# Reordered sums on POOL, one tap moved off PE in every other tile, and the clamps moved to ACT, in the first stage of a fused vision block

## The chip, the cores and the metric

The kernel runs on one core of one Trainium2 chip. The metric is the device time of one execution in microseconds (us). An execution has a span, from the first to the last recorded instruction, and a slightly longer time of its own. Five engines run their instruction streams in parallel, each in program order: PE (TensorE, matmuls into PSUM), DVE (VectorE), ACT (ScalarE), POOL (GpSimd) and SP (which issues the transfers here). They meet only at semaphores: an instruction waits until a counter has reached a value, and adds to another counter when it is done.

## The reference, cut to what matters

The input x has the shape (2, 64, 256, 256): two batches of 64 channels. The change touches only the first stage, which computes the first residual and the input of the recurrent layer behind it:

```
x  = x + depthwise_conv_3x3(_ln_c(x), L0_conv_kernel)      # nine taps per channel, padding 1
t  = _to_tokens(x)                                         # (batch, 65536, 64)
Wx = einsum('bti,hi->bth', _ln_t(t), W)                    # then batch-norm statistics of Wx
```

Here `_ln_c` and `_ln_t` subtract the mean over the 64 channels of a pixel and divide by the root of the variance over them. Behind this stage come the recurrence, an attention with a 1x1 convolution, a mixture of experts, and the output, which all stay as they are.

## The kernel before, in words

The 128 partitions hold batch times channel, and the free axis holds the pixels. The first stage works in tiles of 512 pixels (two image rows), of which there are NT = 128; four tiles make a block, which is the unit of the loads and of the layer-norm statistics. The stage is a software pipeline written out by hand. Every engine loops over steps t, and in step t it does its part of the tile g = t - lag, with one lag for each part: SQ = -4 (squares of the loaded x), CENTER = 5 (centring matmul, and the scaling on DVE), TAPS = 8 (tap matmuls on PE, tap products on ACT, their sums on POOL), SUMS = 9 (tap sums on DVE), FINISH = 10 (the last sum on POOL, which writes the new x), SQ1 = 10 (squares of the new x on ACT), PROJECT = 18 and SCALE = 19. The order inside a step is the order of the lines of that engine's loop.

The nine taps of the convolution are shared out. Of each tile PE does taps 3, 4 and 5 as matmuls with diagonal matrices into the PSUM tile `pst` (L385). DVE adds taps 6, 7 and 8 (L543), the last one into `acc`. ACT makes the products of taps 0, 1 and 2 in `prod` (named tap_products, L454), one buffer for each of the three, so that the product n of a tile can be written only when POOL has added product n of the tile before. POOL adds the three products to x in the buffer `xr` (named x_and_products, three of them, L485), each sum needing the one in front of it, and then adds `acc` in `finish` (L492), which writes x_ring.

The layer norms take two rounds of statistics per block, one for the loaded x (layer 0) and one for the new x (layer 1): PE means over channels of x and of its square (L368, L374), ACT the square of the mean (L432), DVE variance and clamp at zero (L550, L557), ACT logarithm and exponential, which make the reciprocal root (L439, L443, in the function `rsqrt`). The result goes to DRAM and comes back spread over the channels (L316, L325). A round stands in every second step. In the loop of ACT, `rsqrt` comes first in such a step, then the first product, the square of the mean, the other two products, the square of a loaded tile, and last the square of the new x (`square(1, g)`, L425), which waits for `finish` of the same step:

```
if l == 0:
    act.wait_ge(*loaded_x(k))
else:
    act.wait_ge(x1_ready, g + 1)
```

Of the kernel before, what the change touches and what calls it, by code (L numbers as in the profile page):

```python
# [10 lines left out]
ALU = mybir.AluOpType  # L11
# [11 lines left out]
NT = N // TILE  # L23
# [44 lines left out]
def build_program(nc, x, conv_k, ffn_w, ffn_v, gamma, beta, q_w, q_b, kv_w, kv_b, proj_w, proj_b,  # L68
# [4 lines left out]
    with stack:  # L73
# [144 lines left out]
        with ExitStack() as ph:  # L218
# [1 line left out]
            XSLOTS = 8  # L220
            RT = 8
            XR = 3
            NP, ND = len(ACT_TAPS), len(DVE_TAPS)
            X = sb("x_ring", [P, XSLOTS, BLOCK], F32, ph)
            xn = sb("xn", [P, 2 * RT + 2, PITCH], F32, ph)
            u = sb("wx", [P, 2, BLOCK], F32, ph)
# [70 lines left out]

            def wide(ps):
                return ps[:, :].rearrange("p (r w) -> p r w", w=W)

            @blk.sync
            def _(sp):
# [52 lines left out]
            @blk.tensor  # L355
            def _(pe):
                def stats_of(l, k):


                    n = round_of[l, k]  # L360
                    if l == 0:
                        pe.wait_ge(*loaded_x(k))
                    else:
                        pe.wait_ge(x1_ready, TPB * (k + 1))
                    if n:
                        pe.wait_ge(msq_done, n)
                    for j in range(TPB):
                        m = pe.matmul(psm[32 * j:32 * j + 32, :], stat32[:, :], x_tile(TPB * k + j), start=True, stop=True)  # L368
                    m.then_inc(mean_ready, 1)
                    pe.wait_ge(squared[l], TPB * (k + 1))  # L370
                    if n:
                        pe.wait_ge(clamped, n)
                    for j in range(TPB):
                        m = pe.matmul(pse[32 * j:32 * j + 32, :], stat32[:, :], sq[l][:, j, :], start=True, stop=True)  # L374
                    m.then_inc(second_ready, 1)

                def tap_sums(g):
                    pe.wait_ge(normed, min(g + 2, NT))
                    pe.wait_ge(pads_ready, 1)
                    if halos[g + 1]:  # L380
                        pe.wait_ge(halo, halos[g + 1])
                    if g >= 2:
                        pe.wait_ge(acc_step, ND * (g - 1))
                    for n, t in enumerate(PE_TAPS):
                        m = pe.matmul(wide(pst[g % 2]), taps[:, n * P:(n + 1) * P], tap_rows(g, t),  # L385
                                      start=(n == 0), stop=(n == len(PE_TAPS) - 1))
                    m.then_inc(taps_ready, 1)

                def center_x(g):
                    k = g // TPB  # L390
                    pe.wait_ge(*loaded_x(k))
                    if g >= 2:
                        pe.wait_ge(normed, g - 1)
                    pe.matmul(psc[g % 2][:, :], center, x_tile(g), start=True, stop=True).then_inc(centered, 1)  # L394

                def project(g):
                    pe.wait_ge(x1_ready, g + 1)
                    if g >= 2:
                        pe.wait_ge(u_ready, g - 1)
                    pe.matmul(psw[g % 2][:, :], wcT[:, :], x_tile(g), start=True, stop=True).then_inc(wx_ready, 1)  # L400

                for t in range(0, STEPS_A):
                    for l in range(2):
                        if (k := block_at(t, STATS[l])) is not None:
                            stats_of(l, k)
                    if (g := tile_at(t, CENTER)) is not None:
                        center_x(g)
                    if (g := tile_at(t, TAPS)) is not None:
                        tap_sums(g)
                    if (g := tile_at(t, PROJECT)) is not None:  # L410
                        project(g)

            @blk.scalar
            def _(act):
# [18 lines left out]

                def rsqrt(l, k):
                    n = round_of[l, k]
                    act.wait_ge(clamped, n + 1)
                    if n:
                        act.wait_ge(rstd_ready, n)
                    act.activation(ln[:, :], var[:, :], ACT.Ln, bias=(eps_c, eps_t)[l]).then_inc(ln_done, 1)  # L439
                    act.wait_ge(ln_done, n + 1)  # L440
                    if n >= 2:
                        act.wait_ge(rstd_out[n % 2], 32 * (n // 2))
                    act.activation(rstd[:, n % 2, :], ln[:, :], ACT.Exp, scale=-0.5).then_inc(rstd_ready, 1)  # L443

                def tap_product(g, n):
                    if n == 0:
                        act.wait_ge(normed, min(g + 2, NT))
                        act.wait_ge(pads_ready, 1)
                        if halos[g + 1]:
                            act.wait_ge(halo, halos[g + 1])  # L450
                    if g >= 1:
                        act.wait_ge(product_added, NP * (g - 1) + n + 1)
                    t = ACT_TAPS[n]
                    act.activation(prod[:, n, :, :], tap_rows(g, t), ACT.Copy,  # L454
                                   scale=kk[:, t:t + 1]).then_inc(products, 1)
# [19 lines left out]
            @blk.gpsimd  # L475
            def _(pool):
                pool.memset(xn[:, :, :].rearrange("p r w -> p (r w)"), 0.0).then_inc(pads_ready, 1)

                def add_product(g, n):
                    if n == 0 and g >= XR:  # L480
                        pool.wait_ge(x1_ready, g - XR + 1)
                    pool.wait_ge(products, NP * g + n + 1)
                    if n:
                        pool.wait_ge(product_added, NP * g + n)
                    pool.tensor_tensor(xr[:, g % XR, :], prod[:, n, :, :].rearrange("p r w -> p (r w)"),  # L485
                                       xr[:, g % XR, :] if n else x_tile(g), ALU.add).then_inc(product_added, 1)

                def finish(g):

                    pool.wait_ge(product_added, NP * (g + 1))  # L490
                    pool.wait_ge(acc_step, ND * (g + 1))
                    pool.tensor_tensor(x_tile(g), acc[:, g % 2, :, :].rearrange("p r w -> p (r w)"),  # L492
                                       xr[:, g % XR, :], ALU.add).then_inc(x1_ready, 1)

                for t in range(TAPS, STEPS_A):
                    if (g := tile_at(t, FINISH)) is not None:
                        finish(g)
                    if (g := tile_at(t, TAPS)) is not None:
                        for n in range(NP):
                            add_product(g, n)  # L500

            @blk.vector
            def _(dve):
                dve.wait_ge(pads_ready, 1)

                def norm_x(g):
# [3 lines left out]
                    if g >= RT:  # L510
                        done = g - RT + 2
                        dve.wait_ge(taps_ready, done)
                        dve.wait_ge(products, NP * done)
                        dve.wait_ge(acc_step, ND * done)
                    ps, scale = wide(psc[g % 2]), rb[0][:, k % 2, cols_of(g % TPB)].rearrange("p (r w) -> p r w", w=W)
                    if q == 0 and g:
                        dve.tensor_tensor(xn[:, 2 * RT + 1, 1:W + 1], ps[:, 0, :], scale[:, 0, :], ALU.mult).then_inc(halo, 1)
# [4 lines left out]
                def below_the_last_row():  # L522
                    done = NT - RT
                    dve.wait_ge(taps_ready, done)
                    dve.wait_ge(products, NP * done)
                    dve.wait_ge(acc_step, ND * done)
                    dve.memset(xn[:, 2 * RT + 1, 1:W + 1], 0.0).then_inc(halo, 1)

                def tap(g, n):
# [3 lines left out]
                        if halos[g + 1]:  # L533
                            dve.wait_ge(halo, halos[g + 1])
                    else:
                        dve.wait_ge(acc_step, ND * g + n)
                    out = wide(pst[g % 2])
                    if n == ND - 1:
                        if g >= 2:
                            dve.wait_ge(x1_ready, g - 1)  # L540
                        out = acc[:, g % 2, :, :]
                    t = DVE_TAPS[n]
                    dve.scalar_tensor_tensor(out=out, in0=tap_rows(g, t), scalar=kk[:, t:t + 1], in1=wide(pst[g % 2]),  # L543
                                             op0=ALU.mult, op1=ALU.add).then_inc(acc_step, 1)

                def variance(l, k):
# [1 line left out]
                    dve.wait_ge(second_ready, n + 1)  # L548
                    dve.wait_ge(msq_done, n + 1)
                    dve.tensor_tensor(pse[:, :], pse[:, :], msq[:, :], ALU.subtract).then_inc(var_done, 1)  # L550

                def clamp(l, k):
                    n = round_of[l, k]
                    dve.wait_ge(var_done, n + 1)
                    if n:
                        dve.wait_ge(ln_done, n)
                    dve.tensor_scalar(var[:, :], pse[:, :], 0.0, None, ALU.max).then_inc(clamped, 1)  # L557

                def scale_wx(g):
                    k = g // TPB  # L560
# [15 lines left out]
                for t in range(0, STEPS_A):  # L576
# [11 lines left out]
                        tap(g, 1)  # L588
                    if (g2 := tile_at(t, SCALE + TPB)) is not None:
                        statistics(g2)  # L590
                    for l, k in rounds:
                        clamp(l, k)
                    if g is not None:
                        tap(g, 2)
                    if (g := tile_at(t, CENTER)) is not None:
                        norm_x(g)


        with ExitStack() as ph:
# [1340 lines left out]
```

## Time and profile before

| | us |
|---|---|
| median of three runs | 1922.44 (1921.51 to 1926.3) |
| time of the profiled execution | 1924.74 |
| its span | 1922.9 |
| first product sum of tile 2 to that of tile 127, both on POOL | 666.0 |
| first stage, until its last instruction on DVE or ACT | about 757 |

A busy share of an engine over the span mixes stages with different limits, so this change is read from the stretch in which the first stage runs evenly, from about 50 to 725 us, and from single steps inside it. A granted clock of 1.00 is TensorE's full 2.4 GHz, and 0.50 is 1.2 GHz; a value between them is a mean over the stretch.

### The profile page before, as it was taken

How to read it: one execution, taken by the hardware profiler on the slowest of the kernel's cores; microseconds unless marked ns; L12 is line 12 of the kernel's file. 1: busy time of each engine (PE TensorE's matmuls, PEld its weight loads, DVE VectorE, ACT ScalarE, POOL GpSimd, SP SyncE). 2: the span in 40 equal slices, each digit the busy share in tenths (PEclk: the TensorE clock that was granted, in tenths of full speed). 3: DMA queues.
4: the chain of work that ended last, by engine and by line, in shares of the span. 5: the costliest groups of instructions: out<-in, count | busy, mean ns of one | idle time of the engine just before them, and what ended most of it. 6: DMA issues, size and time to landing. Idle time of an engine off the chain costs nothing. (4 is left out here: it accounts for less than half of the span.)

```text
span 1922.9 us, 24399 instructions
## 1 busy us (share of the span) xinstructions
PE 1556.5 (81%) x5627; PEld 648.4 (34%) x5627; DVE 1435.2 (75%) x2312; ACT 1238.3 (64%) x2178; POOL 1450.8 (75%) x1070
## 2 busy tenths in 40 slices
PE   4899999999999993698886679999999999816100
PEld 1333333333333331365553333333333333206000
DVE  1689999999999985498887547999999999951000
ACT  2777777777777751487875458889888888610000
POOL 2999999999999991058787129999999999901670
PEclk8999999999999996799988779999999999955555
DMA  4578888887888664989996527888888887570111
GB/s 152 163 230 254 251 234 256 251 254 234 253 254 252 192 192 152 313 278 373 368 391 269 219 45 209 287 287 287 285 284 275 278 286 246 192 179 13 2 2 1
DMA packets 114478, 429.81 MB, mean 224 GB/s; under 512 B 46720, under 2 KB 51744, under 8 KB 69280
## 3 DMA queue, kind: packets, MB, share of 16 engines
q1 hardware_dynamic: 92656, 423.78, 69.1%
q10 hardware_dynamic: 18736, 4.29, 1.5%
q8 instruction: 49, 0.80, 0.2%
q0 software_dynamic: 2944, 0.18, 0.1%
q14 instruction: 93, 0.76, 0.1%
HBM read 257.89 MB, written 170.01 MB: 223 GB/s over the span
## 5 line engine op out<-in xcount | busy, mean ns | idle before, releaser
L454 ACT ACTIVATE tap_products<-xn,kk 128x512 f32<-128x512 f32 x384 | 275.0, 718 | 156.6 <-POOL x_and_products L485 149.4
L485 POOL TENSOR_TENSOR x_and_products<-tap_products,x_and_products 128x512 f32<-128x512 f32 x256 | 327.1, 1278 | 41.5 <-POOL x_and_products L485 3.5
L385 PE MATMUL pst<-xn,taps 128*128 128x512 f32 x768 | 351.2, 592 | 0.0
L913 DVE SCALAR_TENSOR_TENSOR pss<-region,bn,pss 128x256 f32<-128x256 f32 x432 | 196.3, 489 | 67.4 <-PE pss L807 64.8
L1495 POOL TENSOR_SCALAR exp_q<-exp_q 128x512 f32<-128x512 f32 x128 | 189.3, 1479 | 73.3 <-ACT exp_q L1446 73.3
L852 POOL TENSOR_TENSOR x_block<-x_block,region 128x2048 f32<-128x2048 f32 x28 | 155.3, 5545 | 110.8 <-ACT region L839 88.5
L543 DVE SCALAR_TENSOR_TENSOR pst<-xn,kk,pst 128x512 f32<-128x512 f32 x256 | 192.2, 751 | 60.4 <-PE pst L385 60.2
L385 PEld LDWEIGHTS pst<-xn,taps 128*128 128x128 f32 x768 | 145.3, 189 | 186.3 <-issue 186.1
L1490 POOL TENSOR_TENSOR sq_norm<-x_ring 128x512 f32<-128x512 f32 x128 | 188.6, 1473 | 5.6 <-DVE x_ring L1542 1.7
L485 POOL TENSOR_TENSOR x_and_products<-tap_products,x_ring 128x512 f32<-128x512 f32 x128 | 163.4, 1277 | 19.2 <-ACT tap_products L454 19.2
L425 ACT ACTIVATE sq<-x_ring 128x512 f32<-128x512 f32 x256 | 157.6, 622 | 16.7 <-POOL x_ring L492 10.1
L1502 POOL TENSOR_TENSOR q_z<-q_map,z_inv 128x512 f32<-128x512 f32 x128 | 163.9, 1281 | 0.0
L492 POOL TENSOR_TENSOR x_ring<-acc,x_and_products 128x512 f32<-128x512 f32 x128 | 163.3, 1276 | 0.0
L807 PE MATMUL pss<-region,vT 128*128 128x256 f32 x480 | 137.5, 411 | 18.4 <-ACT region L839 18.2
L568 DVE TENSOR_TENSOR wx<-psw,rstd_wide 128x512 f32<-128x512 f32 x128 | 137.4, 1073 | 17.1 <-DMA rstd_wide<-rstd_scratch 10.9
L1379 PE MATMUL ps_denominator<-q_map,dT 128*128 128x512 f32 x256 | 138.5, 623 | 9.7 <-DVE q_map L1536 8.4
L1373 PE MATMUL ps_query<-x_ring,qcT 128*128 128x512 f32 x256 | 140.4, 632 | 4.0 <-DVE query L1527 4.0
L394 PE MATMUL psc<-x_ring,cst 128*128 128x512 f32 x256 | 140.1, 630 | 3.4 <-DVE xn L520 3.4
L400 PE MATMUL psw<-x_ring,wcT 128*128 128x512 f32 x256 | 132.9, 603 | 11.6 <-DVE wx L568 11.6
L807 PE MATMUL pss<-warm_state,vT 128*128 128x256 f32 x352 | 108.5, 431 | 40.2 <-ACT warm_state L839 22.1
L839 ACT ACTIVATE region<-pss,bn 128x256 f32<-128x256 f32 x256 | 116.6, 474 | 29.4 <-DVE pss L913 28.7
L1452 ACT ACTIVATE ln_d<-ps_denominator,cols 128x512 f32<-128x512 f32 x128 | 86.8, 678 | 73.2 <-PE ps_denominator L1379 73.0
(246 smaller groups left out, 2954.1 us busy)
## 6 DMA issues: line engine op xcount, KB each, us to landing
rstd_wide<-rstd_scratch SPq DMA_DIRECT2D x128, 512.0 KB, 7.2
x_ring<-in_x SPq DMA_DIRECT2D x32, 1024.0 KB, 5.3
x_scratch<-x_ring SPq DMA_DIRECT2D x32, 1024.0 KB, 4.3
xl_scratch<-wx SPq DMA_DIRECT2D x32, 1024.0 KB, 8.7
region<-xl_scratch SPq DMA_DIRECT2D x32, 1024.0 KB, 11.4
x_ring<-x_scratch SPq DMA_DIRECT2D x32, 1024.0 KB, 5.3
rstd_of_channels<-rstd_scratch SPq DMA_DIRECT2D x64, 512.0 KB, 7.5
out<-x_ring SPq DMA_DIRECT2D x32, 1024.0 KB, 6.6
```

The costliest lines, as they stand in the source:

```text
L385: m = pe.matmul(wide(pst[g % 2]), taps[:, n * P:(n + 1) * P], tap_rows(g, t), start=(n == 0), stop=(n == len(PE_TAPS) - 1))
L425: act.activation(sq[l][:, g % TPB, :], x_tile(g), ACT.Square).then_inc(squared[l], 1)
L454: act.activation(prod[:, n, :, :], tap_rows(g, t), ACT.Copy, scale=kk[:, t:t + 1]).then_inc(products, 1)
L485: pool.tensor_tensor(xr[:, g % XR, :], prod[:, n, :, :].rearrange("p r w -> p (r w)"), xr[:, g % XR, :] if n else x_tile(g), ALU.add).then ...
L492: pool.tensor_tensor(x_tile(g), acc[:, g % 2, :, :].rearrange("p r w -> p (r w)"), xr[:, g % XR, :], ALU.add).then_inc(x1_ready, 1)
L543: dve.scalar_tensor_tensor(out=out, in0=tap_rows(g, t), scalar=kk[:, t:t + 1], in1=wide(pst[g % 2]), op0=ALU.mult, op1=ALU.add).then_inc(a ...
L807: pe.matmul(ps_at(r, j), vT[:, :], before, start=True, stop=True).then_inc(carried, 1)
L852: pool.tensor_tensor(in_chunks(x1_x2), in_chunks(x1_x2), y, ALU.add).then_inc(added, 1)
L913: dve.scalar_tensor_tensor(out=ps_at(r, j), in0=u, scalar=gain_w, in1=ps_at(r, j), op0=ALU.mult, op1=ALU.add).then_inc(summed, 1)
L1490: pool.tensor_tensor(sq[1][:, g % SQSLOTS[1], :], x_tile(g), x_tile(g), ALU.mult).then_inc(squared[1], 1)
L1495: pool.tensor_scalar(e, e, 1.0, None, ALU.min).then_inc(clipped, 1)
L1502: pool.tensor_tensor(qz[:, g % 2, :], qm[:, g % QSLOTS, :], zr[:, g % 2, :], ALU.mult).then_inc(qz_ready, 1)
```

## The change

On POOL, a step now reads: first product of tile t-8, third product of tile t-9, second product of tile t-8, and then `finish` of tile t-10. Before, `finish` of tile t-10 stood first, and the three products of tile t-8 followed. ACT's waits for a free product buffer and POOL's waits for its own sums go by the new order of counting (`added_no`). In odd tiles PE does only taps 3 and 4, and DVE does taps 5, 6, 7 and 8, the fourth behind `norm_x`. The clamp of the variance moves from DVE to ACT, as a Relu at the head of `rsqrt`. The order of the rest of ACT's loop, the lags and the buffers stay.

```diff
+            added_no = {}
+            for g in range(NT + 1):
+                for tile, n in ((g, 0), (g - 1, 2), (g, 1)):
+                    if 0 <= tile < NT:
+                        added_no[tile, n] = len(added_no) + 1
+
+            def pe_taps(g):
+                return PE_TAPS[:2] if g % 2 else PE_TAPS
+
+            def dve_taps(g):
+                return PE_TAPS[2:] + DVE_TAPS if g % 2 else DVE_TAPS
...
                 def rsqrt(l, k):
                     n = round_of[l, k]
+                    act.wait_ge(var_done, n + 1)
+                    if n:
+                        act.wait_ge(ln_done, n)
+                    act.activation(var[:, :], pse[:, :], ACT.Relu).then_inc(clamped, 1)
                     act.wait_ge(clamped, n + 1)
...
                     if g >= 1:
-                        act.wait_ge(product_added, NP * (g - 1) + n + 1)
+                        act.wait_ge(product_added, added_no[g - 1, n])
...
                     if n:
-                        pool.wait_ge(product_added, NP * g + n)
+                        pool.wait_ge(product_added, added_no[g, n - 1])
...
                 for t in range(TAPS, STEPS_A):
+                    if (g := tile_at(t, TAPS)) is not None:
+                        add_product(g, 0)
+                    if (g := tile_at(t, TAPS + 1)) is not None:
+                        add_product(g, 2)
+                    if (g := tile_at(t, TAPS)) is not None:
+                        add_product(g, 1)
                     if (g := tile_at(t, FINISH)) is not None:
                         finish(g)
-                    if (g := tile_at(t, TAPS)) is not None:
-                        for n in range(NP):
-                            add_product(g, n)
...
-                def clamp(l, k):
-                    n = round_of[l, k]
-                    dve.wait_ge(var_done, n + 1)
-                    if n:
-                        dve.wait_ge(ln_done, n)
-                    dve.tensor_scalar(var[:, :], pse[:, :], 0.0, None, ALU.max).then_inc(clamped, 1)
...
-                    for l, k in rounds:
-                        clamp(l, k)
                     if g is not None:
                         tap(g, 2)
-                    if (g := tile_at(t, CENTER)) is not None:
-                        norm_x(g)
+                    if (g3 := tile_at(t, CENTER)) is not None:
+                        norm_x(g3)
+                    if g is not None and len(dve_taps(g)) == 4:
+                        tap(g, 3)
```

## Rows read from the trace of the kernel before

**Rows 1.** The windows view: busy us of each engine, granted clock, DMA.
```profile
100.00:200.00 100.00, 100.00 (x335) 38.95 (x334) 90.06 (x133) 76.58 (x122) 94.41 (x76) 1.00 0.82 240
```
**Rows 2.** The timeline of POOL: start, us, engine, line and operation.
```profile
55.33 1.27 POOL L485 TENSOR_TENSOR x_and_products<-tap_products,x_ring 128x512 f32<-128x512 f32 x1
...
86.33 1.27 POOL L492 TENSOR_TENSOR x_ring<-acc,x_and_products 128x512 f32<-128x512 f32 x1
87.56 1.27 POOL L485 TENSOR_TENSOR x_and_products<-tap_products,x_ring 128x512 f32<-128x512 f32 x1
88.98 1.27 POOL L485 TENSOR_TENSOR x_and_products<-tap_products,x_and_products 128x512 f32<-128x512 f32 x1
90.39 1.27 POOL L485 TENSOR_TENSOR x_and_products<-tap_products,x_and_products 128x512 f32<-128x512 f32 x1
91.61 1.28 POOL L492 TENSOR_TENSOR x_ring<-acc,x_and_products 128x512 f32<-128x512 f32 x1
...
721.35 1.28 POOL L485 TENSOR_TENSOR x_and_products<-tap_products,x_ring 128x512 f32<-128x512 f32 x1
```
**Rows 3.** The view of waits from 100 to 700 us: total, times, longest.
```profile
ACT tap_products L454 <- POOL x_and_products L485: 133.1, 212, 0.9
DVE pst L543 <- PE pst L385: 47.1, 56, 1.9
...
ACT sq L425 <- POOL x_ring L492: 3.6, 7, 0.5
```
**Rows 4.** The timeline of PE: one centring (x2) and one tile's taps (x6).
```profile
309.19 1.13 PE L394 MATMUL psc<-x_ring,cst 128*128 128x512 f32 x2
310.15 2.74 PE L385 MATMUL pst<-xn,taps 128*128 128x512 f32 x6
```
**Rows 5.** The timeline of ACT, two steps; x2 is two in a row.
```profile
71.08 1.23 ACT L425 ACTIVATE sq<-x_ring 128x512 f32<-128x512 f32 x2
72.22 0.71 ACT L439 ACTIVATE ln<-var,cols 128x512 f32<-128x512 f32 x1
72.96 0.63 ACT L443 ACTIVATE rstd<-ln 128x512 f32<-128x512 f32 x1
73.50 0.71 ACT L454 ACTIVATE tap_products<-xn,kk 128x512 f32<-128x512 f32 x1
74.11 0.58 ACT L432 ACTIVATE mean_squared<-ps_mean 128x512 f32<-128x512 f32 x1
```
**Rows 6.** The timeline where ACT releases POOL, and a square ahead of a product.
```profile
42.77 0.72 ACT L454 ACTIVATE tap_products<-xn,kk 128x512 f32<-128x512 f32 x1 [3.68 <-DVE xn L520]
43.57 1.26 POOL L485 TENSOR_TENSOR x_and_products<-tap_products,x_ring 128x512 f32<-128x512 f32 x1 [19.25 <-ACT tap_products L454]
47.81 0.62 ACT L425 ACTIVATE sq<-x_ring 128x512 f32<-128x512 f32 x1
48.33 1.32 ACT L454 ACTIVATE tap_products<-xn,kk 128x512 f32<-128x512 f32 x2
```
**Rows 7.** The timeline near the stage's end, where POOL's last sum releases ACT.
```profile
714.84 1.27 POOL L492 TENSOR_TENSOR x_ring<-acc,x_and_products 128x512 f32<-128x512 f32 x1
716.14 0.63 ACT L425 ACTIVATE sq<-x_ring 128x512 f32<-128x512 f32 x1 [0.50 <-POOL x_ring L492]
```
**Rows 8.** The lines view, 100 to 700 us: the clamp.
```profile
L557 DVE TENSOR_SCALAR var<-ps_second 128x512 f32<-128x512 f32 x56 | 37.9, 676 | 0.0
```
**Rows 9.** The timeline of the stage's tail: the last round but one.
```profile
722.71 0.63 ACT L443 ACTIVATE rstd<-ln 128x512 f32<-128x512 f32 x1
732.81 1.03 DVE L568 TENSOR_TENSOR wx<-psw,rstd_wide 128x512 f32<-128x512 f32 x1 [4.20 <-DMA rstd_wide<-rstd_scratch]
```
**Rows 10.** The windows view where PE is not always busy.
```profile
745.00:750.00 5.00, 2.16 (x3) 1.10 (x4) 3.06 (x5) 0.00 (x0) 0.00 (x0) 0.50 0.57 215
960.00:980.00 20.00, 14.22 (x54) 10.32 (x54) 17.41 (x31) 12.27 (x28) 14.96 (x5) 0.83 1.01 378
```

More of the change, by code:

```diff
@@ L222, in build_program @@
             XR = 3
-            NP, ND = len(ACT_TAPS), len(DVE_TAPS)
+            NP = len(ACT_TAPS)
             X = sb("x_ring", [P, XSLOTS, BLOCK], F32, ph)
@@ L299, in wide, with acc_steps @@
                 return ps[:, :].rearrange("p (r w) -> p r w", w=W)
+            added_no = {}
[7 more added lines that the diff above has]
+                return PE_TAPS[2:] + DVE_TAPS if g % 2 else DVE_TAPS
+            def acc_steps(tiles):
+                return sum(len(dve_taps(g)) for g in range(tiles))
             @blk.sync
@@ L382, in tap_sums @@
                     if g >= 2:
-                        pe.wait_ge(acc_step, ND * (g - 1))
-                    for n, t in enumerate(PE_TAPS):
+                        pe.wait_ge(acc_step, acc_steps(g - 1))
+                    for n, t in enumerate(pe_taps(g)):
                         m = pe.matmul(wide(pst[g % 2]), taps[:, n * P:(n + 1) * P], tap_rows(g, t),
-                                      start=(n == 0), stop=(n == len(PE_TAPS) - 1))
+                                      start=(n == 0), stop=(n == len(pe_taps(g)) - 1))
                     m.then_inc(taps_ready, 1)
@@ L488, in finish @@
                 def finish(g):
-                    pool.wait_ge(product_added, NP * (g + 1))
-                    pool.wait_ge(acc_step, ND * (g + 1))
+                    pool.wait_ge(product_added, added_no[g, NP - 1])
+                    pool.wait_ge(acc_step, acc_steps(g + 1))
                     pool.tensor_tensor(x_tile(g), acc[:, g % 2, :, :].rearrange("p r w -> p (r w)"),
@@ L513, in norm_x @@
                         dve.wait_ge(products, NP * done)
-                        dve.wait_ge(acc_step, ND * done)
+                        dve.wait_ge(acc_step, acc_steps(done))
                     ps, scale = wide(psc[g % 2]), rb[0][:, k % 2, cols_of(g % TPB)].rearrange("p (r w) -> p r w", w=W)
@@ L525, in below_the_last_row @@
                     dve.wait_ge(products, NP * done)
-                    dve.wait_ge(acc_step, ND * done)
+                    dve.wait_ge(acc_step, acc_steps(done))
                     dve.memset(xn[:, 2 * RT + 1, 1:W + 1], 0.0).then_inc(halo, 1)
@@ L535, in tap @@
                     else:
-                        dve.wait_ge(acc_step, ND * g + n)
+                        dve.wait_ge(acc_step, acc_steps(g) + n)
                     out = wide(pst[g % 2])
-                    if n == ND - 1:
+                    if n == len(dve_taps(g)) - 1:
                         if g >= 2:
@@ L541, in tap @@
                         out = acc[:, g % 2, :, :]
-                    t = DVE_TAPS[n]
+                    t = dve_taps(g)[n]
                     dve.scalar_tensor_tensor(out=out, in0=tap_rows(g, t), scalar=kk[:, t:t + 1], in1=wide(pst[g % 2]),
```

## The prediction, made before the changed kernel was run

> **What bounds the kernel now.** I read four views, in this order. The windows view shows how full each engine is while the first stage runs evenly [rows 1]: PE is busy for all of 100 us at the full clock, POOL for 94.4, DVE for 90.1, ACT for only 76.6. Two engines are candidates. The timeline of POOL then shows what the 5.6 us that are not busy are made of [rows 2]. `finish` at 86.33 and the sum behind it at 87.56 lie 1.23 us apart, so independent sums follow each other at that pitch. The sums at 87.56, 88.98 and 90.39, each needing the one in front, lie 1.42 and 1.41 us apart: a dependence costs 0.19 us. A tile is thus 1.23 + 1.42 + 1.41 + 1.22 = 5.28 us on POOL with no slack anywhere. From the first sum of tile 2 (55.33) to that of tile 127 (721.35) it is 666.0 us for 125 tiles, 5.33 each [rows 2]. POOL sets the pace; PE, whose busy share is full, stands close behind and is no slower than 5.33 per tile.
>
> The third view is the waits [rows 3]. ACT's products waited for POOL 212 times, 133.1 us together: ACT has slack, and it stands in front of the products. The wait that matters below is the small one: ACT's square of the new x waited for POOL's `finish` 7 times in 600 us, 3.6 us together. It was cheap because `finish` opened POOL's step. The fourth view, ACT's timeline, gives the prices of the pieces.
>
> **The change part by part.**
>
> *The order on POOL.* Only pairs that follow directly pay the 0.19. In the new order none of the four sums needs the product sum in front of it; the first sum of tile g still waits until `finish` of tile g-3 has freed its buffer, and that is now the instruction directly ahead. By itself a step would be 3 x 1.23 + 1.42 = 5.11 us, a gain of 0.22 on 5.33, or 27 us over 125 tiles. That gain needs a POOL that never waits for ACT.
>
> *What the order does to ACT.* Here I follow one loop through both programs. POOL's step ends with `finish` of tile g-2. ACT's step ends with the square of that same tile, which waits for it. ACT is in order, so the first product of tile g+1 stands behind that square, and POOL has nothing to do until it is there. Before, `finish` of g-2 was done before the first sum of tile g, some 4 us earlier, and this path had slack. Now the path is closed with no slack:
>
> - first sum to the end of `finish`: three pitches of 1.23 and one duration of 1.27 [rows 2], 4.96 us;
> - `finish` to the square: it ends at 714.84 + 1.27 = 716.11 and the square starts at 716.14 [rows 7], 0.03;
> - square to the product behind it: 47.81 to 48.33 [rows 6], 0.52;
> - product: 0.72, and release of POOL from 42.77 + 0.72 = 43.49 to 43.57 [rows 6], 0.08.
>
> Sum: 6.31 us for a step in which ACT has nothing else there. POOL idles 1.35 of them.
>
> *The statistics inside that loop.* `rsqrt` opens ACT's step in every second step, between the square and the product, so in the new order it lies on the path too. The second square of the pair at 71.08 starts at about 71.69 and the logarithm at 72.22, so 0.53; logarithm to exponential 72.22 to 72.96, 0.74; exponential to product 72.96 to 73.50, 0.54 [rows 5]. The Relu in front of it reads PSUM as the square of the mean does (0.58 [rows 5]) and its result is waited for as the exponential waits for the logarithm (0.03), so 0.61. Square to product becomes 0.53 + 0.61 + 0.74 + 0.54 = 2.42 instead of 0.52, which adds 1.90 us; such a step takes 8.21. No Relu is in the trace of before. Its lower bound is the 0.52 at which a square passes on [rows 6], its upper the 0.72 of a product; I take 0.58, the row that reads the same PSUM shape. Before, the clamp stood on DVE (676 ns each [rows 8]) off the path.
>
> *The sum over the stage.* The loop acts between the first sum of tile 2 and that of tile 127, 125 times. The steps 11 to 135 hold 29 rounds of layer 0 (steps 14, 18, ... 126) and 30 of layer 1 (16, 20, ... 132), so 59 `rsqrt`. That is 125 x 6.31 + 59 x 1.90 = 788.8 + 112.1 = 900.9 us against 666.0: +234.9.
>
> *The tail.* The `rsqrt` of the last round but one stands in step 136. Before it ended at 722.71 + 0.63 = 723.34, 1.99 us after the last tile's first sum, and the chain of transfer and scaling hangs on it (732.81, released by the transfer [rows 9]). Now it comes behind the square of tile 125: 4.96 + 0.03 + 0.53 + 0.61 + 0.74 + 0.63 = 7.50 us after that sum. The tail is 5.5 us longer. In the last round nothing precedes the Relu, and leaving DVE's order gives back some 0.6. I take +5.
>
> *The other parts.* Moving a tap costs nothing here, and gains nothing. DVE gets one tap and loses one clamp per two tiles; at 90% of 5.33 us per tile [rows 1] it does about 4.8 us of work in a step of 7.2. PE loses two matmuls per two tiles, (2.74 - 1.13) / 4 = 0.40 each [rows 4]: at most 10.66 - 0.80 = 9.86 us of work in 14.4. The cover for both is the loop above; without it DVE and PE would each set some 5 us per tile. The new wait on ACT holds back the products and, in every second step, PE's second-moment matmuls, which need the Relu of the round before; PE's taps of that step are used by DVE a step later and by POOL two steps later, which leaves several us.
>
> Prediction: 1924.74 + 234.9 + 5 = 2164.6, say 2165 us. The profiled execution lies 2.3 above the median, which the range covers.
>
> **Weighing the clock.** With PE a third idle, its clock can fall. The row nearest to that load is 960 to 980 us: busy 14.22 of 20, granted clock 0.83 [rows 10]; at 745 to 750, busy 2.16 of 5, it was 0.50. At 0.83, 9.86 us of work take 11.9, still inside 14.4. The Trainium skill (TensorE: Matmul & The Clock Gate, Part 1) says that the throttled state is the default and that activity lifts it. By the row the sum stays 2165; by that rule, taken to its end, see the second rival.
>
> **The rivals.**
>
> *Slower than that: PE at half clock becomes the bound.* The two tiles' 9.86 us double to 19.7 if every matmul runs at 1.2 GHz, and 62.5 pairs make 1232 us, +566, so 2496. It decides from the point where more than 14.4 / 9.86 - 1 = 46% of PE's work is done at the low level. At 60% the pair takes 15.8 and the total is 2250. For it: PE will pause in every pair of tiles. Against it: a PE that is behind stops pausing, and at such loads the clock stays above 0.8 [rows 10]. The skill's rule above names this cause.
>
> *Slower, but less: only the third product closes a loop.* It waits for a sum that now stands behind the first sum of the next tile: 1.23 + 1.27 + 0.03 + 0.62 (product to square) + 2 x 0.52 + 0.72 + 0.08 = 4.99, under POOL's 5.11, and 6.89 with `rsqrt`. 66 x 5.11 + 59 x 6.89 = 743.8, with the tail some 2008. This would hold if the square did not wait for `finish` of its own step; both lags are 10, so I see no room for it.
>
> *Faster: the loop doesn't close.* If the products were ready ahead of POOL, the step would be 5.11 and the time 1925 - 27 = 1898. It decides where the first product is made before `finish` ends. For it speak only ACT's 23% of idle time [rows 1] and the small wait of the square [rows 3]; against it, that this wait was small because of the very order that changes.
>
> **How the numbers follow.** Loop through `finish` as summed, 0.84, own range 2148 to 2210: the low end takes off 0.1 per step for releases that overlap more, the high end adds 0.1 for a square that passes on at a product's pitch (0.62), 0.09 for a slower release, 0.14 for each Relu, and up to 15 for pauses behind a slower PE. Half-clock PE 0.06, third product only 0.04, faster 0.04, no change 0.02. My range is 2142 to 2215. The chances below are those of faster by over 0.3%, within 0.3%, and slower by over 0.3%, which is about the smallest step that a measurement of this kernel tells from no change.
>
> **What would show it.** Right: POOL's busy share in the even stretch at some 70%, with an idle of 1.35 us before the first sum of each tile, and 3.25 in every second one, released by ACT's product; ACT's square released by POOL's `finish` some 125 times, 1.2 us each; first sum of tile 2 to tile 127 about 901 us; nothing changed behind the stage but its start. Wrong: first sums 5.1 us apart (no loop), or 5.1 and 6.9 (third product), or POOL idle behind DVE's `acc` with a granted clock of 0.6 or less (PE). An idle time well over 1.35 without `rsqrt` would mean that a release or the pitch of ACT is mis-sized.

## The result, and the profile after

The changed kernel takes 2171.21 us (median of four executions, 2165.34 to 2171.81), against 1924.37 (four executions) for the kernel before. The ratio is 1.1275, with a 95% interval of 1.1257 to 1.1294. It was forecast at 2165, with a range of 2142 to 2215. The profiled execution took 2171.58 us at a span of 2169.8.

In the code of the changed kernel the lines of the stage are L505 (the three product sums on POOL), L512 (the last sum), L474 (tap products on ACT), L441 (squares), L455 (the Relu), L459 and L463 (logarithm and exponential) and L566 (DVE's taps). The timeline of POOL answers to [rows 2]; in brackets stands the idle time ahead and who ended it.

```profile
56.42 1.27 POOL L505 TENSOR_TENSOR x_and_products<-tap_products,x_ring 128x512 f32<-128x512 f32 x1 [2.62 <-ACT tap_products L474]
...
303.58 1.27 POOL L505 TENSOR_TENSOR x_and_products<-tap_products,x_ring 128x512 f32<-128x512 f32 x1 [3.32 <-ACT tap_products L474]
304.80 2.50 POOL L505 TENSOR_TENSOR x_and_products<-tap_products,x_and_products 128x512 f32<-128x512 f32 x2
307.26 1.26 POOL L512 TENSOR_TENSOR x_ring<-acc,x_and_products 128x512 f32<-128x512 f32 x1
309.94 1.28 POOL L505 TENSOR_TENSOR x_and_products<-tap_products,x_ring 128x512 f32<-128x512 f32 x1 [1.42 <-ACT tap_products L474]
311.18 2.51 POOL L505 TENSOR_TENSOR x_and_products<-tap_products,x_and_products 128x512 f32<-128x512 f32 x2
313.62 1.28 POOL L512 TENSOR_TENSOR x_ring<-acc,x_and_products 128x512 f32<-128x512 f32 x1
318.23 1.28 POOL L505 TENSOR_TENSOR x_and_products<-tap_products,x_ring 128x512 f32<-128x512 f32 x1 [3.32 <-ACT tap_products L474]
...
965.45 1.28 POOL L505 TENSOR_TENSOR x_and_products<-tap_products,x_ring 128x512 f32<-128x512 f32 x1 [1.42 <-ACT tap_products L474]
```

The dependences between neighbouring sums are gone, as intended: the two sums that make up an "x2" take 2.50 us together, 1.23 from start to start, where a pair took 2.68 before (88.98 to 91.66 in [rows 2]). In exchange POOL now idles ahead of every first sum, 1.42 us in one step and 3.32 in the next. A step is 6.36 us or 8.29 us. From tile 2 to tile 127 it is 909.0 us, against 666.0.

ACT's timeline over the same two steps shows what POOL waits for; it answers to [rows 5].

```profile
306.10 0.72 ACT L474 ACTIVATE tap_products<-xn,kk 128x512 f32<-128x512 f32 x1 [1.57 <-POOL x_and_products L505]
306.73 0.61 ACT L441 ACTIVATE sq<-x_ring 128x512 f32<-128x512 f32 x1
308.56 0.63 ACT L441 ACTIVATE sq<-x_ring 128x512 f32<-128x512 f32 x1 [1.22 <-POOL x_ring L512]
309.10 1.32 ACT L474 ACTIVATE tap_products<-xn,kk 128x512 f32<-128x512 f32 x2
...
314.94 0.63 ACT L441 ACTIVATE sq<-x_ring 128x512 f32<-128x512 f32 x1 [1.22 <-POOL x_ring L512]
315.48 0.58 ACT L455 ACTIVATE var<-ps_second 128x512 f32<-128x512 f32 x1
316.09 0.72 ACT L459 ACTIVATE ln<-var,cols 128x512 f32<-128x512 f32 x1
316.85 0.63 ACT L463 ACTIVATE rstd<-ln 128x512 f32<-128x512 f32 x1
317.38 0.71 ACT L474 ACTIVATE tap_products<-xn,kk 128x512 f32<-128x512 f32 x1
```

Follow one turn. POOL's last sum ends at 307.26 + 1.26 = 308.52. The square starts at 308.56, the first product at 309.10, it ends at 309.82, and POOL starts at 309.94. In the other kind of step, Relu, logarithm and exponential stand between square (314.94) and product (317.38). ACT waits for POOL and POOL waits for ACT, in turn, and neither is full: the windows view, which answers to [rows 1], and the view of waits from 100 to 900 us, which answers to [rows 3].

```profile
100.00:200.00 100.00, 76.85 (x232) 26.79 (x231) 64.42 (x94) 57.66 (x95) 67.83 (x55) 0.89 0.56 169
500.00:600.00 100.00, 77.53 (x234) 27.20 (x233) 67.37 (x100) 58.25 (x97) 67.79 (x55) 0.88 0.60 180
```

```profile
POOL x_and_products L505 <- ACT tap_products L474: 257.2, 109, 3.3
ACT tap_products L474 <- POOL x_and_products L505: 200.5, 110, 2.1
...
ACT sq L441 <- POOL x_ring L512: 133.1, 109, 1.7
```

The square's wait was met 7 times in 600 us before and 109 times in 800 us now, once in every step. No engine is above 80% busy: the time is the sum of a chain that runs through POOL and ACT, a closed loop.

### The profile page after: what moved, and what is told of

Same layout as the page of the kernel before. It is cut to its first block and busy times, and to the rows that moved or that the text cites. A ratio compares the mean times of both kernels' runs of the same rounds, so it can differ in the third digit from the quotient of the medians.

```text
span 2169.8 us, 24207 instructions
## 1 busy us (share of the span) xinstructions
PE 1606.5 (74%) x5499; PEld 642.0 (30%) x5499; DVE 1441.5 (66%) x2312; ACT 1260.9 (58%) x2242; POOL 1442.8 (66%) x1070
## 5 line engine op out<-in xcount | busy, mean ns | idle before, releaser
L474 ACT ACTIVATE tap_products<-xn,kk 128x512 f32<-128x512 f32 x384 | 267.1, 712 | 235.5 <-POOL x_and_products L505 231.2
L505 POOL TENSOR_TENSOR x_and_products<-tap_products,x_ring 128x512 f32<-128x512 f32 x128 | 162.8, 1272 | 312.5 <-ACT tap_products L474 312.5
L505 POOL TENSOR_TENSOR x_and_products<-tap_products,x_and_products 128x512 f32<-128x512 f32 x256 | 320.4, 1274 | 2.7 <-ACT tap_products L474 2.7
L401 PE MATMUL pst<-xn,taps 128*128 128x512 f32 x640 | 312.2, 619 | 2.0 <-DVE acc L566 2.0
L566 DVE SCALAR_TENSOR_TENSOR pst<-xn,kk,pst 128x512 f32<-128x512 f32 x320 | 239.1, 747 | 90.9 <-PE pst L401 90.4
L441 ACT ACTIVATE sq<-x_ring 128x512 f32<-128x512 f32 x256 | 158.5, 622 | 167.2 <-POOL x_ring L512 160.9
L543 DVE TENSOR_TENSOR xn<-psc,rstd_wide 128x512 f32<-128x512 f32 x128 | 87.9, 688 | 163.4 <-PE psc L410 156.9
L401 PEld LDWEIGHTS pst<-xn,taps 128*128 128x128 f32 x640 | 133.2, 209 | 186.1 <-issue 181.6
L390 PE MATMUL ps_second<-sq,stat 128*32 128x512 f32 x512 | 106.3, 914 | 109.8 <-ACT var L455 102.4
L410 PE MATMUL psc<-x_ring,cst 128*128 128x512 f32 x256 | 173.3, 766 | 4.6 <-DVE xn L543 4.6
L512 POOL TENSOR_TENSOR x_ring<-acc,x_and_products 128x512 f32<-128x512 f32 x128 | 162.7, 1271 | 0.9 <-DVE acc L566 0.9
L384 PE MATMUL ps_mean<-x_ring,stat 128*32 128x512 f32 x512 | 83.2, 727 | 106.2 <-POOL x_ring L512 99.3
L416 PE MATMUL psw<-x_ring,wcT 128*128 128x512 f32 x256 | 135.7, 616 | 10.7 <-DVE wx L584 10.7
```

Of the source, the lines that this page charges most:

```text
L441: act.activation(sq[l][:, g % TPB, :], x_tile(g), ACT.Square).then_inc(squared[l], 1)
L474: act.activation(prod[:, n, :, :], tap_rows(g, t), ACT.Copy, scale=kk[:, t:t + 1]).then_inc(products, 1)
```

## The experiments

Kernels sent together ran on the same chip beside the kernel before, whose medians there were 1925.6 to 1927.1 us. The "stretch" is always from the first product sum of tile 2 to that of tile 127 on POOL, in the profiled execution.

**1. The last sum back at the head of POOL's step.**

```diff
+                    if (g := tile_at(t, FINISH)) is not None:
+                        finish(g)
                     if (g := tile_at(t, TAPS)) is not None:
                         add_product(g, 0)
...
-                    if (g := tile_at(t, FINISH)) is not None:
-                        finish(g)
```

> The changed kernel with the last sum back at the head of POOL's step; nothing else is edited. Theory (two loops, the outer one through the last sum and the square of the same tile, and inside it a second one through the third product): the outer loop opens, the inner one takes over, 1.23 + 1.27 + 0.03 + 0.62 + 0.52 + 0.54 + 0.72 + 0.10 = 5.03 us between first sums, and 6.95 with the statistics; 66 x 5.03 + 59 x 6.95 = 742 us from tile 2 to tile 127, so about 2000 us. Rival (the place of the last sum was the whole cost): POOL's four independent sums set the pace at 4 x 1.23 = 4.92, 615 us, about 1875. Rival (PE's clock or its later start is the cause of the slow stage): about 2171 as it is.

Measured: 2004.23 us, ratio 1.0401 (1.0384 to 1.0418). The stretch is 741.7 us against 742 forecast. Two thirds of the loss are the place of the last sum. The rest is the second loop, through the third product. POOL's third sum frees its buffer, the third product and two squares follow on ACT, and only then the next first product. The timeline of this kernel shows it in steps of 5.05 and 6.95 us:

```profile
309.80 0.72 ACT L474 ACTIVATE tap_products<-xn,kk 128x512 f32<-128x512 f32 x1 [1.59 <-POOL x_and_products L505]
310.42 1.13 ACT L441 ACTIVATE sq<-x_ring 128x512 f32<-128x512 f32 x2
311.47 1.32 ACT L474 ACTIVATE tap_products<-xn,kk 128x512 f32<-128x512 f32 x2
312.31 1.27 POOL L505 TENSOR_TENSOR x_and_products<-tap_products,x_ring 128x512 f32<-128x512 f32 x1
...
319.26 1.26 POOL L505 TENSOR_TENSOR x_and_products<-tap_products,x_ring 128x512 f32<-128x512 f32 x1 [1.99 <-ACT tap_products L474]
...
324.31 1.28 POOL L505 TENSOR_TENSOR x_and_products<-tap_products,x_ring 128x512 f32<-128x512 f32 x1
```

**2. The square of the new x a whole step later**, with POOL's order as changed.

```diff
-            SQ, CENTER, TAPS, SUMS, FINISH, SQ1, PROJECT, SCALE = -4, 5, 8, 9, 10, 10, 18, 19
+            SQ, CENTER, TAPS, SUMS, FINISH, SQ1, PROJECT, SCALE = -4, 5, 8, 9, 10, 11, 18, 19
```

> The changed kernel with the square of the new x one step later (SQ1 = 11), so that it never waits for a sum of its own step; POOL's order stays as changed. Theory: only the inner loop through the third product is left, under POOL's own 5.11: 66 x 5.11 + 59 x 6.95 = 747 us, with the longer tail about 2010; up to 2030 if PE, whose second-moment matmuls of the new x now wait for a square of their own step, falls behind. Rival (the closed loop isn't through this square): no change, 2171.

Measured: 2147.17 us, ratio 1.1147 (1.1125 to 1.1169), stretch 876.8. A miss: I had 747 for the stretch. Three steps of four did come as forecast, 406.21 to 411.28 (5.07), to 418.23 (6.95), to 423.27 (5.04), but the fourth lasted until 435.48, 12.21 us. The timeline, the windows view and the waits of this kernel show what took it:

```profile
406.00 1.04 PE L390 MATMUL ps_second<-sq,stat 128*32 128x512 f32 x8
...
410.50 1.02 PE L416 MATMUL psw<-x_ring,wcT 128*128 128x512 f32 x2
...
422.57 1.94 PE L390 MATMUL ps_second<-sq,stat 128*32 128x512 f32 x8 [5.21 <-ACT sq L441]
...
429.98 1.02 PE L416 MATMUL psw<-x_ring,wcT 128*128 128x512 f32 x2
...
435.48 1.28 POOL L505 TENSOR_TENSOR x_and_products<-tap_products,x_ring 128x512 f32<-128x512 f32 x1 [6.18 <-ACT tap_products L474]
```

```profile
420.00:425.00 5.00, 2.43 (x9) 0.70 (x10) 0.00 (x0) 2.99 (x5) 4.91 (x5) 0.50 0.98 301
```

```profile
PE ps_second L390 <- ACT sq L441: 144.0, 28, 5.2
ACT var L455 <- DVE ps_second L573: 122.2, 28, 5.2
```

One square in four is the last of its block, and PE's second-moment matmuls wait for it at the head of PE's step while ACT now makes it at the end of its own. PE stands 5.2 us, the taps and the next variance on DVE come later, and two steps on ACT stands at the Relu for up to 5.2 us. I had allowed 20 us for this; it cost 130. PE's clock has a part in it: behind the pause it was granted 0.50, and from the second-moment matmuls to the projection (L416) PE took 7.41 us, 422.57 to 429.98, against 4.50 one round earlier, 406.00 to 410.50. DVE's scaling of Wx, the variance and the Relu stand behind that projection. An estimate from this one round is that some 2.9 of the 12.21 us are the lowered clock's, and by the 30 steps of over 10 us at most 87 of the 130; no run separates it. So this run tells that another loop was closed, and does not tell by itself that the first was opened.

**3. The same idea without that side effect**: the square behind the first product of the next step.

```diff
                     if g is not None:
                         tap_product(g, 0)
+                    if (g1 := tile_at(t, SQ1 + 1)) is not None:
+                        square(1, g1)
...
-                    if (g := tile_at(t, SQ1)) is not None:
-                        square(1, g)
```

> The changed kernel with ACT's square of the new x moved behind the first product of the next step (it then reads a tile whose last sum ended before that product was even needed); POOL's order stays as changed, last sum at the end. Unlike the square a whole step later, PE gets the square near the head of its step, so that its second-moment matmuls and DVE's variance aren't late. Theory: the outer loop opens though POOL still sums last; the inner one is shorter by the square, 1.23 + 1.27 + 0.03 + 0.62 + 0.54 + 0.72 + 0.10 = 4.51, under POOL's own 5.11, and 6.43 with the statistics: 66 x 5.11 + 59 x 6.43 = 717 us for the stretch, about 1985 us. Rival (what made the square a step later slow, 2147, is any delay of this square): 2100 or more. Rival (a last sum at the end of POOL's step is slow in itself): about 2171.

Measured: 1984.44 us, ratio 1.0302 (1.0275 to 1.0329), stretch 720.7 against 717 forecast. POOL still sums last, as in the changed kernel; only one instruction on ACT has another place, and 187 us are gone. This is the run that names the cause. Its timeline shows product and square in their new order:

```profile
314.19 0.71 ACT L474 ACTIVATE tap_products<-xn,kk 128x512 f32<-128x512 f32 x1
314.20 1.28 POOL L512 TENSOR_TENSOR x_ring<-acc,x_and_products 128x512 f32<-128x512 f32 x1
...
315.51 0.63 ACT L441 ACTIVATE sq<-x_ring 128x512 f32<-128x512 f32 x1 [0.61 <-POOL x_ring L512]
315.56 1.27 POOL L505 TENSOR_TENSOR x_and_products<-tap_products,x_ring 128x512 f32<-128x512 f32 x1
```

The square still waits for POOL's last sum, but the product that POOL needs is done before it, and POOL goes on 0.08 us after that sum. The 3% that are left lie in the steps with statistics, where POOL still waits for ACT (68.9 us in 43 waits from 100 to 600 us). That the stretch came out so near to the forecast is in part luck: the 66 plain steps took 5.05 us on the mean, not 5.11, and the 59 others 6.57, not 6.43.

**4. The clamp back on DVE**, all else as changed (the Relu's lines leave `rsqrt`, `clamp` and its call return to DVE).

```diff
-                    act.activation(var[:, :], pse[:, :], ACT.Relu).then_inc(clamped, 1)
...
+                    for l, k in rounds:
+                        clamp(l, k)
```

> The changed kernel with the clamp back on DVE. Theory: the Relu stands on the path in 59 steps at 0.61 us each, so 36 us less: 2135. Rival (the statistics are off the path, the plain loop is all): within 3 us of 2171. Rival (DVE is the bound, which would get 0.6 us more in every second step): slower than 2171 by up to 40.

Measured: 2135.45 us, ratio 1.1086 (1.1064 to 1.1108), stretch 872.2. The long steps lose 0.63 us each (2.69 us of idle time instead of 3.32), the short ones nothing: 59 x 0.63 = 37.

**5. POOL's order alone**, all else as in the kernel before. Against the changed kernel that is the edit of 4 and, shown here, three taps on PE in every tile.

```diff
-                return PE_TAPS[:2] if g % 2 else PE_TAPS
+                return PE_TAPS
...
-                return PE_TAPS[2:] + DVE_TAPS if g % 2 else DVE_TAPS
+                return DVE_TAPS
```

> The kernel before with only POOL's order and the waits that go with it changed: clamp on DVE, taps 3, 4 and 5 on PE in every tile. Theory: PE and DVE are covered by the loop, so the moved tap is worth nothing here: 66 x 6.37 + 59 x 7.68 = 874 us for the stretch, about 2136 us, as the kernel with the clamp back. Rival (PE bounds the slow stage): slower than that by up to 62 x 0.86 = 53 us.

Measured: 2138.43 us, ratio 1.1101 (1.1079 to 1.1124), stretch 872.0, the same as in 4 within 0.3 us. Two matmuls more or less on PE, and a tap more or less on DVE, have no weight under the loop.

**6. More work for PE** in the changed kernel: each centring matmul is issued twice.

```diff
+                    pe.matmul(psc[g % 2][:, :], center, x_tile(g), start=True, stop=True)
                     pe.matmul(psc[g % 2][:, :], center, x_tile(g), start=True, stop=True).then_inc(centered, 1)
```

> The changed kernel with each centring matmul issued twice, which gives PE two more matmul instructions of 0.43 us per tile (at the full clock) and changes no result. Theory (the loop of POOL and ACT sets the pace and covers PE): within 8 us of 2171, with PE busier and its granted clock the same or higher. Rival (PE, at a lowered clock, is part of what bounds the slow stage): up to 128 x 0.86 = 110 us slower.

Measured: 2173.93 us, ratio 1.1286 (1.1256 to 1.1316), stretch 909.5 against 909.0. The windows view of this kernel shows that PE took the work, at a higher granted clock than the 0.86 of the changed kernel in the same stretch:

```profile
300.00:400.00 100.00, 85.74 (x259) 32.38 (x256) 66.84 (x99) 59.03 (x98) 66.84 (x55) 0.93 0.60 182
```

In the changed kernel PE's idle time and its lowered clock are consequences of the loop, not a part of it.

**7 to 9. The other two edits without the order**, on the kernel before: the tap alone, the clamp alone, and both. Shown is POOL's order put back in the changed kernel, which gives "both"; "tap alone" has the edit of 4 besides, and "clamp alone" is the kernel before with the Relu's lines on ACT.

```diff
-                for tile, n in ((g, 0), (g - 1, 2), (g, 1)):
+                for tile, n in ((g, 0), (g, 1), (g, 2)):
...
+                    if (g := tile_at(t, FINISH)) is not None:
+                        finish(g)
+                    if (g := tile_at(t, TAPS)) is not None:
+                        for n in range(NP):
+                            add_product(g, n)
```

> The kernel before with only the tap moved in odd tiles (PE two taps, DVE four); POOL's and ACT's order and the clamp as before. Theory: POOL set the pace before, 5.28 by its own instructions against 5.33 measured, so 0 to 6 us faster: 1919 to 1926. Rival (PE was the bound): 0.86 us per two tiles, up to 50 us faster. Rival (DVE becomes the bound with the extra tap): slower.

> The kernel before with only the clamp moved to ACT. Theory: ACT has slack in that order, so within 3 us of before; but PE's second-moment matmuls now wait for ACT, and if ACT gets to the Relu late, PE, busy all the time, loses what it waits: up to 10 us slower. Rival (a Relu on ACT costs its 0.61 us wherever it is): 36 us slower.

> The changed kernel with POOL's order as before: tap moved and clamp on ACT, but not the reordered sums. Theory: the order is the whole loss, and the other two edits together give what they give alone: 1917 to 1928. Rival (the three edits are slow only together): 1950 or more.

| | us | ratio, 95% | stretch |
|---|---|---|---|
| tap alone | 1924.64 | 0.9991 (0.9980 to 1.0001) | 666.1 |
| clamp alone | 1925.20 | 0.9990 (0.9980 to 0.9999) | 665.9 |
| both | 1923.53 | 0.9972 (0.9956 to 0.9988) | 666.0 |

The stretch does not move by more than 0.1 us from the 666.0 of before, so the 0.3% by which "both" lies below 1 was not gained there. With the tap moved PE is no longer always busy, and POOL is as full as in [rows 1]; the windows view of the run with the tap alone:

```profile
500.00:600.00 100.00, 93.38 (x321) 35.33 (x318) 96.69 (x146) 76.74 (x124) 94.40 (x76) 1.00 0.82 247
```

So POOL alone set the pace of the kernel before, and a PE that is busy 100% of the time was not its bound. Without the new order of sums the two other edits lose nothing. With it the moved tap still costs nothing, and the Relu some 33 to 36 us (2171.2 against the 2138.4 and 2135.5 of runs 5 and 4).

**10. ACT's order fitted to POOL's**: last sum at the head as in 1, and ACT's step in another order.

```diff
-                    for l in range(2):
-                        if (k := block_at(t, STATS[l] + 2)) is not None:
-                            rsqrt(l, k)
                     g = tile_at(t, TAPS)
                     if g is not None:
                         tap_product(g, 0)
+                    for l in range(2):
+                        if (k := block_at(t, STATS[l] + 2)) is not None:
+                            rsqrt(l, k)
...
                     if g is not None:
                         tap_product(g, 1)
-                        tap_product(g, 2)
-                    if (g := tile_at(t, SQ)) is not None:
-                        square(0, g)
-                    if (g := tile_at(t, SQ1)) is not None:
-                        square(1, g)
+                    if (g0 := tile_at(t, SQ)) is not None:
+                        square(0, g0)
+                    if (g1 := tile_at(t, SQ1)) is not None:
+                        square(1, g1)
+                    if g is not None:
+                        tap_product(g, 2)
```

> The changed kernel with POOL's last sum at the head of its step and ACT's step put in the order first product, statistics, square of the mean, second product, the two squares, third product. Theory: between the third product and the next first product nothing is left, so the inner loop is 1.23 + 1.27 + 0.03 + 0.62 + 0.72 + 0.10 = 3.97 us and the statistics have slack until the second product is needed; POOL sets the pace at 4 x 1.23 = 4.92, with PE at most at 4.93: 125 x 4.92 = 615 us, some 50 less than before, about 1877 us (1870 to 1895). Rival (the new order of sums on POOL is of no use at all): 1925 or more.

Measured: 1900.87 us, ratio 0.9864 (0.9842 to 0.9885), stretch 639.2, or 5.11 us per tile. 1.4% faster than before, but outside my 1870 to 1895. POOL hardly waits for ACT any more (0.9 us in three waits); what is left is in the waits of this kernel from 100 to 600 us:

```profile
DVE pst L567 <- PE pst L401: 18.3, 37, 1.2
POOL x_ring L513 <- DVE acc L567: 14.0, 37, 0.7
PE ps_second L390 <- ACT var L455: 11.8, 29, 0.8
```

PE waits for the Relu, which now stands behind the first product; DVE waits for PE, and POOL for DVE.

**11. As 10, with the clamp on DVE.**

> As the run with ACT's new order, with the clamp back on DVE. Theory: ACT has slack in that order, so the clamp on ACT is worth what it saves DVE, whose share was 90 of 100 us at 5.33 per tile (4.8 us of work): within 0 to 12 us of that run, slower if DVE now sets the pace. Rival (the Relu on ACT is on the path there too, as it was in the changed kernel): up to 36 us faster than that run.

Measured: 1895.37 us, ratio 0.9834 (0.9812 to 0.9855), stretch 632.2 or 5.06 per tile. I had expected it 0 to 12 us slower than 10. It is 5 us faster by the medians, with intervals of the ratios that overlap, and 7.0 us shorter in the stretch of the one profiled execution. PE's second-moment matmuls waited 5.6 us for DVE's clamp where in 10 they waited 11.8 for ACT's Relu (both from 100 to 600 us); that this is the reason is likely, not shown. DVE is full now; the windows view of this kernel:

```profile
300.00:400.00 100.00, 98.48 (x337) 35.40 (x336) 100.00 (x153) 76.39 (x127) 97.24 (x80) 1.00 0.90 265
```

**12. As 10, with the Relu alone ahead of the first product.**

```diff
+                    for l in range(2):
+                        if (k := block_at(t, STATS[l] + 2)) is not None:
+                            relu(l, k)
                     g = tile_at(t, TAPS)
                     if g is not None:
                         tap_product(g, 0)
```

> The run with ACT's new order (last sum at the head of POOL's step), with the Relu alone put back ahead of the first product; logarithm and exponential stay behind it. Theory (what kept that run at 5.11 us per tile is a ring of PE, which waits for the Relu before its second-moment matmuls, DVE, and POOL's last sum, which waits for DVE): PE's waits for the Relu go, the inner loop becomes 3.97 + 0.6 = 4.6 and stays under 4.92, and the stage runs at 4.95 to 5.05 per tile: 8 to 20 us under that run's 1901, 1881 to 1893. Rival (DVE's own work sets the 5.11): no change, 1901.

Measured: 1885.06 us (five executions, 1884.01 to 1886.79), ratio 0.9779 (0.9765 to 0.9792), as forecast. The stretch is 622.8 us, 4.98 per tile, close to the 4.92 of four independent sums. POOL's timeline and the windows view of this kernel:

```profile
313.64 1.29 POOL L519 TENSOR_TENSOR x_ring<-acc,x_and_products 128x512 f32<-128x512 f32 x1
314.88 1.28 POOL L512 TENSOR_TENSOR x_and_products<-tap_products,x_ring 128x512 f32<-128x512 f32 x1
316.11 2.52 POOL L512 TENSOR_TENSOR x_and_products<-tap_products,x_and_products 128x512 f32<-128x512 f32 x2
318.59 1.27 POOL L519 TENSOR_TENSOR x_ring<-acc,x_and_products 128x512 f32<-128x512 f32 x1
```

```profile
300.00:400.00 100.00, 98.81 (x341) 36.52 (x340) 98.29 (x147) 80.77 (x140) 98.68 (x81) 1.00 0.89 265
```

PE, DVE and POOL are now all at 98% or more. All three edits of the change are in this kernel, the fastest of all. What the clamp's place is worth here depends on ACT's order: on ACT it gains 10 us against run 11 when the Relu stands ahead of the first product, and none when it stands behind it (run 10). What the moved tap is worth here was not run. An estimate: one tap less in two tiles saves PE two matmuls, 0.40 us per tile by [rows 4], and PE, 98.8% busy in a step of 4.98, has 0.06 to spare.

## Why the prediction was right

*The pace before.* Right: POOL's own instructions. The runs 7 to 9 show it more strictly than [rows 1] could, since PE stood at 100 there too. POOL's own waits in the kernel before, from 100 to 700 us, say the same; this is the whole view, and no other engine is in it:

```profile
POOL x_and_products L485 <- POOL x_and_products L485: 3.0, 7, 0.4
```

*The loop through the last sum.* Right in mechanism, shown by runs 1 and 3 from its two ends, POOL's order and ACT's order. Its size was 6.36 us instead of 6.31. Each release of ACT by POOL took 0.04 instead of 0.03, square to product 0.54 instead of 0.52, and the release of POOL by ACT 0.12 instead of the 0.08 of [rows 6]. On the mean of its 66 steps without statistics it was 6.37, and some 0.06 x 125 = 8 us come from there. Where POOL does not wait for ACT, its own step was 5.05 and not the 5.11 of the prediction (run 3): from the last sum to the next first sum it took 1.36, not 1.42. The forecast did not use that term; two of the rivals did.

*The statistics inside the loop.* 318.23 - 309.94 = 8.29 against 6.36 makes 1.93 us in this pair, 1.91 on the mean of all steps, forecast 1.90. From square to product it is 317.38 - 314.94 = 2.44 instead of 0.54. The Relu, which no row of before showed, took 0.58 us as taken from the square of the mean, and 0.63 on the path by run 4.

*The count and the sum.* Forecast +234.9 for the stretch, measured 909.0 - 666.0 = +243.0. The tail is 5.2 us longer (40.94 against 35.74 from the last tile's first sum to the aggregation of the statistics), forecast 5. The start cost 1.1 (56.42 instead of 55.33), which I had left out, and what lies behind the stage was 2.4 shorter. Together 243.0 + 5.2 + 1.1 - 2.4 = 246.9, the difference of the two spans, 2169.8 - 1922.9. The forecast of 2165 is thus 6 us low, mostly by the releases. Of the range, the terms that the prediction names give 2152 at the low end and 2212 at the high end, where it says 2148 and 2210; 2171 lies inside either.

*Tap and clamp at nothing for PE and DVE.* Right: under the loop by runs 5 and 6, and in the kernel before by 7 to 9.

*The rivals.* Half-clock PE, the first of them, is out by run 6. In the pauses the clock did fall, and the windows view of the changed kernel in steps of 5 us shows it:

```profile
300.00:305.00 5.00, 3.45 (x10) 1.07 (x11) 1.72 (x3) 4.17 (x7) 1.68 (x3) 0.59 0.03 10
...
310.00:315.00 5.00, 3.57 (x13) 1.30 (x13) 4.90 (x9) 1.72 (x4) 4.91 (x4) 1.00 0.55 121
```

Here PE had stood idle for 3.03 us until 301.55. The clock was 0.59 on the mean of the first five us, near 1.2 GHz, and back at 2.4 GHz from 310 on; over 100 us it was granted 0.86 to 0.89, where I had taken 0.83 from [rows 10]. The Trainium skill (TensorE: Matmul & The Clock Gate, Part 1) says that the clock is throttled by default and released by activity; the trace agrees, at 0.59 behind a pause and 1.00 ten us later, and in the changed kernel nothing followed for the time. In run 2 the lowered clock did lie on the path. The loop through the third product alone is not what the changed kernel does, but it exists: run 1 shows it once the outer one is open, in steps of 5.05 and 6.95 us against the 4.99 and 6.89 of the prediction. The loop that doesn't close was not seen with this order of ACT; runs 10 to 12 are what it takes.

## What to carry to other kernels

When instructions of one in-order engine are reordered, look for the instruction that now comes last, who waits for it, and what stands behind that waiter in its own queue; if this leads back to the head of the first engine's next step, the step becomes the length of the whole chain, however idle the engines are. A saving of 0.2 us per tile on the busiest engine turned into a loss of 1.9 this way, and one instruction moved within ACT's queue took three quarters of it back (188 of 243 us of the stretch). Where every engine is below 80% and two of them release each other in turn, as here, add up the chain, not the busy shares; and try an edit that looks worthless under one bound (the clamp here, by runs 11 and 12) again once that bound is gone.

## What the runs showed that I had not expected

- A PE that the profile shows busy for 100 of 100 us at the full clock was not the bound: with two matmuls fewer per two tiles its share fell to 93 and the stretch stayed at 666.1 us.
- The release of POOL by an ACT instruction took 0.12 us in the steady loop, where the one row of before had 0.08; the release of ACT by POOL took 0.04.
- A square later by one step cost 130 us more than its own removal from the loop gave reason to expect (run 2), since a statistic that only every fourth tile needs passes through PE, DVE and ACT before it comes back, and PE, just behind its pause, works at half clock there.
